# Output of a delta rule: products and sums on VectorE alone, loop written out

## The chip, the cores and the metric

One core of a Trainium2 chip runs the whole program. The metric is the device time of one execution in microseconds (us). An engine is named as in the profile: PE is TensorE, DVE is VectorE, ACT is ScalarE, POOL is GpSimd, SP is the queue that starts DMAs.

## What is computed

The program is a chain of four layers, each a mixer and a feed-forward part, over 4096 tokens of 128 channels. The change touches the last mixer only, a delta rule with 16 heads of 64 channels over a sequence of 4 steps (S = 4, indices t and r below) for each of 1024 positions (8 tiles j of 128 partitions). Cut to what matters, the reference does

```
def step(W, inp):
    q_t, k_t, v_t, b_t = inp
    v_old = jnp.einsum('bhd,bhdv->bhv', k_t, W)
    new_v = b_t * (v_t - v_old)
    W = W + jnp.einsum('bhd,bhv->bhdv', k_t, new_v)
    out_t = jnp.einsum('bhd,bhdv->bhv', q_t, W)
    return (W, out_t)
_, outs = lax.scan(step, W0, (qs, ks, vs, bs))
out = SCALE * out / (denominator + EPS)
attn_out = jnp.einsum('sbi,oi->sbo', layer_out, W_o)
x = h + attn_out
```

Since the recurrence has only four steps, the kernel doesn't keep W. It first computes coefficients alpha[t, r] for each token and head from dot products of queries and keys, and then the output of step t as the sum over r <= t of alpha[t, r] times the value v[r]. The last part, values, weighted sums, projection by W_o and the addition to h, is the stage called "out".

## The kernel before: the stage "out"

The work is 8 turns j (JT = 8), one for each tile of 128 partitions, and in each turn 4 units t (S = 4). Sizes: a value tile v[r] is 128 x 1024 fp32 (16 heads x 64).

- Values: TensorE multiplies XT by wv, two matmuls of 512 columns for each r (line 2155), into the PSUM tiles pv; ScalarE copies each into v (line 2186).
- Sums: for unit t, VectorE multiplies v[0] by alpha[t, 0] into acc (line 2223). GpSimd multiplies v[r] by alpha[t, r] for r = 1 to t into the two-deep tile tmp (line 2142), and VectorE adds each product to acc (line 2231). Each of these covers 128 x 1024 elements. In a turn there are 4 first products, 6 products on GpSimd and 6 additions.
- Turn: TensorE transposes acc in 8 pieces into pt (line 2160), ScalarE copies them to lT (line 2194), two copies of 512 columns.
- Projection: TensorE multiplies lT by woT in 8 accumulating matmuls into po (line 2172), and VectorE adds po to its rows of XN, which hold h (line 2213, the helper `finish`).

The loops over j are hardware loops (`Fori`). [...] The helper `pipelined` calls `prepare(j + 1)` ahead of `rest(j)`. Each engine runs its own list in order. In `rest`, TensorE does turn(0), and then for each t turn(t + 1) and the projection of t; all values of the next turn are computed in one block ahead of that. xj for the next turn is copied only when the earlier turn is nearly finished: both the copy and ScalarE's eviction wait with

```
pool.wait_ge(x_done, j * S + (S + 1))
```

while VectorE's additions wait for GpSimd, and GpSimd for a free half of tmp:

```
dve.wait_ge(tmp_ready, j * NPAIR + (k + 1))
pool.wait_ge(ch, j * NPAIR + (k + 1))
```

VectorE does `finish(t - 2)` after the sum of t, and after the last unit of a turn `finish(S - 2)` and `finish(S - 1)`, before it starts the next turn.

Of the kernel before, what the change touches and what calls it, by code (L numbers as in the profile page):

```python
# [15 lines left out]
ALU = mybir.AluOpType  # L16
# [1698 lines left out]
def delta_rule(nc, X, XN, XT, ident, W_qkvb, W_o, ln_g, ln_b):  # L1715
# [30 lines left out]
    with Stage(nc, "delta") as s:  # L1746
# [351 lines left out]
        with Stage(nc, "out") as s1:  # L2098
            v = s1.sb("v", [P, 2, S, NH, D_])
            xj = s1.sb("xj", [P, 2, S, P])  # L2100
            aj = s1.sb("aj", [P, 2, S, S, NH])
            acc = s1.sb("acc", [P, 2, NH, D_])
            tmp = s1.sb("tmp", [P, 2, NH, D_])
# [4 lines left out]
            xj_ready, aj_ready, v_mm, v_ready, tmp_ready, acc_ready, t_mm, lT_ready, out_mm, x_done, ch, chm = (s1.sem(n) for n in (  # L2108
                "xj_ready", "aj_ready", "v_mm", "v_ready", "tmp_ready", "acc_ready", "t_mm", "lT_ready", "out_mm", "x_done", "additions", "firsts"))
            NPAIR = S * (S - 1) // 2  # L2110

            def pipelined(eng, prepare, rest):

                prepare(0, 0)
                with eng.Fori(0, JT // 2 - 1) as j2:
                    for par in range(2):
                        prepare(j2 * 2 + (par + 1), 1 - par)
                        rest(j2 * 2 + par, par)
                prepare(JT - 1, 1)
                rest(JT - 2, 0)  # L2120
                rest(JT - 1, 1)

            with nc.Block() as block:

                @block.gpsimd
                def _(pool):
                    def prepare(j, par):

                        pool.wait_ge(x_done, j * S + (S + 1))
                        nc.gpsimd.tensor_copy(xj[:, par].unsqueeze(2), XTj[:, :, bass.ds(j, 1), :]).then_inc(xj_ready, 1)  # L2130
                        nc.gpsimd.tensor_copy(aj[:, par].rearrange("p t s h -> p (t s) h").unsqueeze(2),
                                              alpha[:].rearrange("p t s j h -> p (t s) j h")[:, :, bass.ds(j, 1), :]).then_inc(aj_ready, 1)

                    def rest(j, par):
                        pool.wait_ge(aj_ready, j + 1)
                        k = 0
                        for t in range(1, S):
                            for r in range(1, t + 1):
                                pool.wait_ge(v_ready, j * 2 * S + (2 * r + 4))

                                pool.wait_ge(ch, j * NPAIR + (k + 1))
                                nc.gpsimd.tensor_tensor(tmp[:, k % 2], v[:, par, r], bcast(aj[:, par, t, r], D_), ALU.mult).then_inc(tmp_ready, 1)
                                k += 1

                    pipelined(pool, prepare, rest)

                @block.tensor
                def _(pe):
                    def prepare(j, par):
                        pe.wait_ge(xj_ready, j + 1)  # L2150
                        for t in range(S):
                            for half in range(2):

                                pe.wait_ge(v_ready, j * 2 * S + (2 * t + half + 1))
                                nc.tensor.matmul(pv[half][:], xj[:, par, t], wv[:, half * GROUP:(half + 1) * GROUP], start=True, stop=True).then_inc(v_mm, 1)

                    def turn(j, t):
                        pe.wait_ge(acc_ready, j * S + (t + 1))
                        for a in range(HD // P):
                            ins = nc.tensor.transpose(pt[t % 2][a // 4][:, (a % 4) * P:(a % 4 + 1) * P],  # L2160
                                                      acc[:, t % 2].rearrange("p h d -> p (h d)")[:, a * P:(a + 1) * P], ident[:])
                        ins.then_inc(t_mm, 1)

                    def rest(j, par):
                        turn(j, 0)
                        for t in range(S):
                            if t + 1 < S:
                                turn(j, t + 1)
                            pe.wait_ge(lT_ready, j * S + (t + 1))
                            pe.wait_ge(x_done, j * S + (t + 2 * S))  # L2170
                            for a in range(HD // P):
                                ins = nc.tensor.matmul(po[t % 2][:, 0:C], lT[:, t % 2, a], woT[:, a], start=(a == 0), stop=(a == HD // P - 1))
                            ins.then_inc(out_mm, 1)

                    pipelined(pe, prepare, rest)

                @block.scalar
                def _(act):
                    act.sem_inc(v_ready, 2)
                    def prepare(j, par):  # L2180

                        act.wait_ge(x_done, j * S + (S + 1))
                        for t in range(S):
                            for half in range(2):
                                act.wait_ge(v_mm, j * 2 * S + (2 * t + half + 1))
                                nc.scalar.activation(v[:, par, t, half * 8:(half + 1) * 8].rearrange("p h d -> p (h d)"), pv[half][:], ACT.Copy).then_inc(v_ready, 1)
# [376 lines left out]
```

## Time and profile before

| what | value |
|---|---|
| median of 3 runs | 4349.28 us (4348.84 to 4349.62) |
| the profiled execution | 4347.39 us |
| its span, first to last instruction | 4345.1 us |
| granted TensorE clock, mean | 0.851 of full speed |
| busy in the span: PE / DVE / ACT / POOL | 3053.7 / 2461.8 / 1169.1 / 912.8 us |
| stretch of the stage "out" in the trace | 3614.2 to 3871.9 us from the span's start |
| busy in that stretch: PE / DVE / ACT / POOL | 169.36 / 146.65 / 72.39 / 134.96 us |

The program runs stage by stage with a barrier of all engines between them, so a stage's length adds straight to the time. The profiled execution lies 2.2 us above its span and 1.9 us below the median. Times in the trace count from the span's start. "Idle before" is time in which the engine stood still ahead of the instructions of a row, and the arrow names what ended it.

### The profile page before, as it was taken

The numbers are of one execution on the slowest core, as the hardware profiler recorded it, in microseconds if no ns is written. First come the engines' busy times: TensorE is split into PE (matmuls) and PEld (weight loads), VectorE is DVE, ScalarE is ACT, GpSimd is POOL, SyncE is SP. The second block draws the span as 40 slices with busy tenths as digits, with TensorE's granted clock in tenths as the row PEclk, the third lists the DMA queues.
The fourth block names the chain that finished last, engine by engine and source line by source line (L and its number), as shares of the span: only waits on it lengthen the run. The fifth ranks groups of instructions, "written<-read, shape, count | busy, mean of one in ns | idle before, by whom it ended". The sixth has DMA issues, their size and how long they took to land. (4 is left out here: it accounts for less than half of the span.)

```text
span 4345.1 us, 37123 instructions
## 1 busy us (share of the span) xinstructions
PE 3053.7 (70%) x10599; PEld 1669.7 (38%) x10607; DVE 2461.8 (57%) x4267; ACT 1169.1 (27%) x1861; POOL 912.8 (21%) x521
## 2 busy tenths in 40 slices
PE   1003499799999749999687767458989975635654
PEld 0002256455555524444344423234444433433221
DVE  6785433422222377777544570257777846666876
ACT  1001233211111113333333103234444422212420
POOL 0000000000000000000132111238989853520000
PEclk7556699899999879999787798769999987876888
DMA  0000000000000146455000201110000000000000
GB/s 24 0 0 0 20 0 0 15 0 0 0 0 0 42 74 143 135 143 136 4 1 0 61 8 50 44 39 0 0 0 1 0 20 0 0 2 0 0 5 19
DMA packets 93888, 107.16 MB, mean 25 GB/s; under 512 B 20555, under 2 KB 54476, under 8 KB 93516
## 3 DMA queue, kind: packets, MB, share of 16 engines
q1 hardware_dynamic: 91724, 101.65, 9.5%
q0 software_dynamic: 2048, 4.20, 0.3%
q8 instruction: 45, 0.74, 0.1%
q14 instruction: 71, 0.58, 0.0%
HBM read 91.78 MB, written 14.02 MB: 24 GB/s over the span
## 5 line engine op out<-in xcount | busy, mean ns | idle before, releaser
L1846 POOL TENSOR_TENSOR dots_pr<-dots_g 128x1536 f32<-128x1536 f32 (+1 forms) x129 | 394.2, 3098 | 122.1 <-DVE dots_g L1951 78.3
L1872 PE MATMUL dots_fold<-dots_pr,all_ident 128*128 128x512 f32 x688 | 325.0, 619 | 2.7 <-ACT dots_pr L1912 2.7
L670 DVE SCALAR_TENSOR_TENSOR attn_sim<-attn_sc,attn_mask 128x512 f32<-128x512 f32 (+3 forms) x256 | 125.9, 492 | 316.9 <-PE attn_sc L600 313.7
L600 PE MATMUL attn_sc<-attn_q,attn_xb 128*128 128x512 f32 (+3 forms) x768 | 295.0, 486 | 0.0
L611 PE MATMUL attn_op<-attn_sim,attn_v 128*128 128x512 f32 (+3 forms) x768 | 295.0, 486 | 0.0
L243 PE MATMUL mix_po<-mix_woT,mix_y 128*128 128x128 f32 x128 | 25.5, 390 | 366.7 <-DVE mix_y L357 366.7
L778 PE MATMUL grp_po<-grp_h,grp_down 128*128 128x512 f32 x512 | 263.2, 596 | 10.2 <-DVE grp_h L888 10.2
L786 PE MATMUL grp_ph<-all_xt,grp_up 128*128 x512 | 261.4, 596 | 1.1 <-ACTq L808 1.1
L1948 DVE TENSOR_TENSOR dots_m<-dots_pu,dots_sg 128x512 f32<-128x512 f32 x256 | 164.7, 686 | 161.3 <-ACT dots_sg L1903 154.5
L816 ACT ACTIVATE grp_r<-grp_ph 128x512 f32<-128x512 f32 x272 | 162.7, 598 | 310.8 <-PE grp_ph L786 298.2
L883 DVE TENSOR_TENSOR grp_t<-grp_r,grp_cb 128x512 f32<-128x512 f32 x256 | 177.2, 692 | 90.5 <-ACT grp_r L816 79.0
L1912 ACT ACTIVATE dots_pr<-dots_pr 128x1536 f32<-128x1536 f32 (+1 forms) x129 | 169.5, 1339 | 158.2 <-POOL dots_pr L1846 158.2
L1859 PE MATMUL dots_pu<-delta_wE,all_xt 128*128 128x264 f32 x512 | 152.2, 429 | 80.6 <-DVE dots_g L1951 79.0
L1846 POOL TENSOR_TENSOR all_xn<-dots_g 128x1536 f32<-128x1536 f32 (+3 forms) x63 | 195.7, 3148 | 18.3 <-PE dots_fold L1872 18.3
L1872 PEld LDWEIGHTS dots_fold<-dots_pr,all_ident 128*128 128x128 f32 x688 | 137.0, 199 | 147.3 <-issue 141.8
L600 PEld LDWEIGHTS attn_sc<-attn_q,attn_xb 128*128 128x128 f32 x768 | 141.0, 190 | 125.7 <-issue 107.1
L888 DVE TENSOR_TENSOR grp_h<-grp_t,grp_r 128x512 f32<-128x512 f32 x256 | 177.0, 692 | 10.2
L611 PEld LDWEIGHTS attn_op<-attn_sim,attn_v 128*128 128x128 f32 x768 | 141.0, 190 | 98.4 <-issue 68.9
L243 PEld LDWEIGHTS mix_po<-mix_woT,mix_y 128*128 128x128 f32 x128 | 24.7, 301 | 370.0 <-issue 370.0
L1859 PEld LDWEIGHTS dots_pu<-delta_wE,all_xt 128*128 128x128 f32 x512 | 102.1, 208 | 164.2 <-DVE dots_g L1951 120.3
L1951 DVE SCALAR_TENSOR_TENSOR dots_g<-dots_m,dots_pu 128x512 f32<-128x512 f32 x256 | 163.4, 680 | 0.0
L1872 PE MATMUL dots_fold<-all_xn,all_ident 128*128 128x512 f32 x336 | 155.9, 608 | 1.2 <-ACT all_xn L1912 1.2
(596 smaller groups left out, 5599.2 us busy)
## 6 DMA issues: line engine op xcount, KB each, us to landing
grp_cb<-grp_combine SPq DMA_DIRECT2D x512, 128.0 KB, 3.2
cap_xs<-cap_zero SPq DMA_DIRECT2D x7, 320.0 KB, 4.3
experts_xe<-cap_xs SPq DMA_DIRECT2D x7, 320.0 KB, 3.3
cap_w<-in_L_ffn_W_dram SPq DMA_DIRECT2D x1, 2048.0 KB
cap_ys<-experts_yo SPq DMA_DIRECT2D x8, 256.0 KB, 2.3
delta_h<-all_xn SPq DMA_DIRECT2D x1, 2048.0 KB
all_xn<-delta_h SPq DMA_DIRECT2D x1, 2048.0 KB, 8.0
out_dram<-all_x SPq DMA_DIRECT2D x1, 2048.0 KB, 8.7
```

What stands on the lines that cost most here:

```text
L600: nc.tensor.matmul(sc[k % SC][:, 0:w], xb[:, m * P:(m + 1) * P], q[:, par, n0:n0 + w], start=True, stop=True).then_inc(s_mm, 1)
L611: ins = nc.tensor.matmul(op[half][:, n0 - half * GROUP:n0 - half * GROUP + w], v[:, par, m], sim[:, par, k, 0:w], start=False, stop=False)
L778: ins = nc.tensor.matmul(po[par][:], w, h[:, (par * NJ + j) % HB], start=(j == 0), stop=(j == NJ - 1))
L786: nc.tensor.matmul(ph[j % 2][:], w, XT[:, bass.ds(g * GROUP, GROUP)], start=True, stop=True).then_inc(up_mm, 1)
L883: tt(t_[:, j % 2], r[:, j % 2], cb[:, j % CB], ALU.mult).then_inc(tch, 1)
L888: tt(h[:, (par * NJ + j) % HB], a[:, j % 2], r[:, j % 2], ALU.mult).then_inc(h_done, 1)
L1846: nc.gpsimd.tensor_tensor(slot[U % SLOTS][:, r0 + i0:r0 + i0 + n], g[:, I % 2, a0:a0 + n, hs], key, ALU.mult).then_inc(pp_ready, 1)
L1859: ins = nc.tensor.matmul(heads(n % 2)[:, q * HQ:(q + 1) * HQ], XTj[:, k // 2, j], wE[:, 1 - k % 2, h0:h0 + HQ], start=True, stop=True)
L1872: ins = nc.tensor.matmul(fold[U % NU][:].rearrange("p (n h f) -> p n h f", h=HQ, f=FW), ident[:], slot[U % SLOTS][:, :, :, f * FW:(f + 1) ...
L1912: nc.scalar.activation(v_, v_, ACT.Relu).then_inc(relu_done, 1)
L1948: tt(m[:, sh], x[..., sh + 1:sh + 1 + D_], sg[:, n % 2], ALU.mult).then_inc(m_ready, 1)
L1951: ins = stt(g[:, I % 2, k, :, sh * D_:(sh + 1) * D_], m[:, sh], 0.0, x[..., 0:D_], ALU.max, ALU.mult)
```

## The change

GpSimd has no work left in the stage: VectorE makes all ten products of a turn from v and alpha directly. For a unit t it first issues the product with v[0] into acc, then all products r = 1 to t into a three-deep tile `part`, and then the additions. The loops over j are written out, so that TensorE reads XT and VectorE reads alpha in place (xj and aj are gone), and every wait compares with a constant. The values of turn j + 1 are no longer a block: two of their matmuls stand behind the transposes of each unit, and the projection of the unit before comes behind those. ScalarE follows the same order. VectorE's `finish(n - 2)` follows each unit n = 4j + t, across the border of turns.

The diff, with the removed loops cut:

```diff
             v = s1.sb("v", [P, 2, S, NH, D_])
-            xj = s1.sb("xj", [P, 2, S, P])
-            aj = s1.sb("aj", [P, 2, S, S, NH])
             acc = s1.sb("acc", [P, 2, NH, D_])
-            tmp = s1.sb("tmp", [P, 2, NH, D_])
+            part = s1.sb("part", [P, S - 1, NH, D_])
...
-                @block.gpsimd
-                def _(pool):
...
-                        nc.gpsimd.tensor_copy(xj[:, par].unsqueeze(2), XTj[:, :, bass.ds(j, 1), :]).then_inc(xj_ready, 1)
...
-                                nc.gpsimd.tensor_tensor(tmp[:, k % 2], v[:, par, r], bcast(aj[:, par, t, r], D_), ALU.mult).then_inc(tmp_ready, 1)
...
                 @block.tensor
                 def _(pe):
+                    def values(j, t):
+                        if j >= JT:
+                            return
+                        for half in range(2):
+                            n = (j * S + t) * 2 + half
+                            if n >= 2:
+                                pe.wait_ge(v_ready, n - 1)
+                            nc.tensor.matmul(pv[half][:], XTj[:, t, j], wv[:, half * GROUP:(half + 1) * GROUP], start=True, stop=True).then_inc(v_mm, 1)
+
+                    def sums(j, t):
+                        n = j * S + t
+                        if n >= 2:
+                            pe.wait_ge(lT_ready, n - 1)
+                        pe.wait_ge(acc_ready, n + 1)
                         for a in range(HD // P):
                             ins = nc.tensor.transpose(pt[t % 2][a // 4][:, (a % 4) * P:(a % 4 + 1) * P],
...
+                    def project(n):
+                        if n < 0:
+                            return
+                        pe.wait_ge(lT_ready, n + 1)
+                        if n >= 2:
+                            pe.wait_ge(x_done, n - 1)
+                        for a in range(HD // P):
+                            ins = nc.tensor.matmul(po[n % 2][:, 0:C], lT[:, n % 2, a], woT[:, a], start=(a == 0), stop=(a == HD // P - 1))
+                        ins.then_inc(out_mm, 1)
+
+                    for t in range(S):
+                        values(0, t)
+                    for j in range(JT):
                         for t in range(S):
...
+                            sums(j, t)
+                            values(j + 1, t)
+                            project(j * S + t - 1)
+                    project(JT * S - 1)
...
                 @block.vector
...
+                    def finish(n):
+                        if n < 0:
+                            return
+                        j, t = divmod(n, S)
+                        dve.wait_ge(out_mm, n + 1)
+                        xt = XN[:, j + t * JT]
+                        tt(xt, po[n % 2][:, 0:C], xt, ALU.add).then_inc(x_done, 1)
+
                     dve.wait_ge(h_in, 16)
...
+                    for j in range(JT):
+                        for t in range(S):
+                            n = j * S + t
+                            dve.wait_ge(v_ready, 2 * (n + 1))
+                            if n >= 2:
+                                dve.wait_ge(t_mm, n - 1)
+                            ins = tt(acc[:, n % 2], v[:, j % 2, 0], bcast(alpha[:, t, 0, j], D_), ALU.mult)
+                            ins.then_inc(acc_first if t else acc_ready, 1)
+                            if n >= 1:
+                                dve.wait_ge(acc_ready, n)
+                            for r in range(1, t + 1):
+                                tt(part[:, r - 1], v[:, j % 2, r], bcast(alpha[:, t, r, j], D_), ALU.mult).then_inc(part_ready, 1)
+                            for r in range(1, t + 1):
+                                k = j * NPART + t * (t - 1) // 2 + r
+                                if r == 1:
+                                    dve.wait_ge(acc_first, j * (S - 1) + t)
                                 else:
...
+                                    dve.wait_ge(added, j * (NPART - S + 1) + (t - 1) * (t - 2) // 2 + r - 1)
+                                dve.wait_ge(part_ready, k)
+                                ins = tt(acc[:, n % 2], acc[:, n % 2], part[:, r - 1], ALU.add)
+                                ins.then_inc(added if r < t else acc_ready, 1)
+                            finish(j * S + t - 2)
+                    finish(JT * S - 2)
+                    finish(JT * S - 1)
```

VectorE's list before, units t = 2 and t = 3 of a turn (out_acc is acc, out_tmp is the product made by GpSimd, all_xn is XN, REGISTER_ALU computes a value to wait for):

```order
L2223 TENSOR_TENSOR out_acc<-out_v,out_aj 128x1024
L2228 REGISTER_ALU
L2230 REGISTER_ALU
L2231 TENSOR_TENSOR out_acc<-out_acc,out_tmp 128x1024
L2234 REGISTER_ALU
L2231 TENSOR_TENSOR out_acc<-out_acc,out_tmp 128x1024
L2234 REGISTER_ALU
L2213 ISA
L2213 TENSOR_TENSOR all_xn<-out_po,all_xn 128x128
```

One product by VectorE stands ahead of the two additions of t = 2, and the finish of an earlier unit behind them.

The same list after the change, from unit t = 3 of one turn to unit t = 1 of the next (out_part is part, delta_alpha is alpha):

```order
L2195 TENSOR_TENSOR out_acc<-out_v,delta_alpha 128x1024
L2200 TENSOR_TENSOR out_part<-out_v,delta_alpha 128x1024 x3
L2208 TENSOR_TENSOR out_acc<-out_acc,out_part 128x1024 x3
L2186 TENSOR_TENSOR all_xn<-out_po,all_xn 128x128
L2195 TENSOR_TENSOR out_acc<-out_v,delta_alpha 128x1024
L2186 TENSOR_TENSOR all_xn<-out_po,all_xn 128x128
L2195 TENSOR_TENSOR out_acc<-out_v,delta_alpha 128x1024
L2200 TENSOR_TENSOR out_part<-out_v,delta_alpha 128x1024
L2208 TENSOR_TENSOR out_acc<-out_acc,out_part 128x1024
L2186 TENSOR_TENSOR all_xn<-out_po,all_xn 128x128
```

Four products stand ahead of three additions, and unit t = 0 is one product between two finishes.

TensorE's list before, in one turn, from the last value matmul:

```order
L2155 MATMUL out_pv<-delta_wv,out_xj 128x512
L2158 ISA
L2160 MATMUL out_pt<-all_ident,out_acc 128x128 x8
L2158 REGISTER_ALU
L2160 MATMUL out_pt<-all_ident,out_acc 128x128 x8
L2170 REGISTER_ALU
L2172 MATMUL out_po<-delta_woT,out_lT 128x128 x8
```

Here no value matmul stands between transposes and projections. After the change each unit repeats three rows:

```order
L2129 MATMUL out_pt<-all_ident,out_acc 128x128 x8
L2121 MATMUL out_pv<-delta_wv,all_xt 128x512 x2
L2140 MATMUL out_po<-delta_woT,out_lT 128x128 x8
L2129 MATMUL out_pt<-all_ident,out_acc 128x128 x8
L2121 MATMUL out_pv<-delta_wv,all_xt 128x512 x2
```

The projection of a unit now stands behind the transposes of the next unit and two value matmuls.

## Rows read from the trace of the kernel before

**Rows 1.** Groups by line, 3614.3 to 3871.9: count | busy us, mean ns | idle.

```profile
L2142 POOL TENSOR_TENSOR out_tmp<-out_v,out_aj 128x1024 f32<-128x1024 f32 x48 | 118.7, 2486 | 60.0 <-DVE out_acc L2231 53.9 <-ACT out_v L2186 6.1
L2231 DVE TENSOR_TENSOR out_acc<-out_acc,out_tmp 128x1024 f32<-128x1024 f32 x48 | 84.8, 1767 | 30.5 <-POOL out_tmp L2142 28.6
L2223 DVE TENSOR_TENSOR out_acc<-out_v,out_aj 128x1024 f32<-128x1024 f32 x32 | 53.1, 1678 | 26.1 <-PE out_pt L2160 17.8 <-ACT out_v L2186 6.6 <-DVE all_xn L2213 1.3
L2213 DVE TENSOR_TENSOR all_xn<-out_po,all_xn 128x128 f32 x32 | 9.3, 292 | 53.0 <-PE out_po L2172 48.6 <-DVE out_acc L2231 4.4
```

**Rows 2.** Waits in the same stretch: us in total, times, longest us.

```profile
PE out_pv L2155 <- POOL out_xj L2130: 64.6, 7, 53.7
DVE all_xn L2213 <- PE out_po L2172: 48.6, 16, 5.1
DVE out_acc L2231 <- POOL out_tmp L2142: 28.6, 15, 2.2
```

**Rows 3.** The tile out_acc: durations of one, min/median/max in ns.

```profile
L2231 DVE TENSOR_TENSOR out_acc<-out_acc,out_tmp x48: 1224/1226/2908, 3625.0 to 3861.4; 128x1024 f32<-128x1024 f32 x48
```

**Rows 4.** Timeline, stage start: start us, us, engine, line, tile [idle <-releaser].

```profile
3615.26 0.61 POOL L2130 COPY out_xj<-all_xt 128x512 f32<-128x512 f32 x1 [76.15 <-DVEq L2203]
3615.93 16.21 PE L2155 MATMUL out_pv<-delta_wv,out_xj 128*128 128x512 f32 x32 [53.67 <-POOL out_xj L2130]
3620.21 1.23 DVE L2223 TENSOR_TENSOR out_acc<-out_v,out_aj 128x1024 f32<-128x1024 f32 x1 [5.98 <-ACT out_v L2186]
```

**Rows 5.** Timeline, one turn j of the loop.

```profile
3717.48 2.77 DVE L2223 TENSOR_TENSOR out_acc<-out_v,out_aj 128x1024 f32<-128x1024 f32 x2
3720.48 0.60 ACT L2186 ACTIVATE out_v<-out_pv 128x512 f32<-128x512 f32 x1 [7.05 <-PE out_pv L2155]
3721.34 0.60 ACT L2186 ACTIVATE out_v<-out_pv 128x512 f32<-128x512 f32 x1 [0.26 <-PE out_pv L2155]
3731.60 1.09 PE L2160 MATMUL out_pt<-all_ident,out_acc 128*128 128x128 f32 x8 [0.61 <-DVEq L2236]
3731.75 0.29 DVE L2213 TENSOR_TENSOR all_xn<-out_po,all_xn 128x128 f32 x1 [0.27 <-DVE out_acc L2231]
3731.96 2.37 DVE L2223 TENSOR_TENSOR out_acc<-out_v,out_aj 128x1024 f32<-128x1024 f32 x1
3732.53 1.95 PE L2172 MATMUL out_po<-delta_woT,out_lT 128*128 128x128 f32 x16
3741.63 1.97 PE L2160 MATMUL out_pt<-all_ident,out_acc 128*128 128x128 f32 x8 [7.15 <-DVEq L2236]
3743.39 4.67 PE L2172 MATMUL out_po<-delta_woT,out_lT 128*128 128x128 f32 x32
3748.21 0.29 DVE L2213 TENSOR_TENSOR all_xn<-out_po,all_xn 128x128 f32 x1 [1.49 <-PE out_po L2172]
3748.93 1.43 DVE L2223 TENSOR_TENSOR out_acc<-out_v,out_aj 128x1024 f32<-128x1024 f32 x1 [0.43 <-DVE all_xn L2213]
```

**Rows 6.** Timeline of VectorE: two or more operations close together.

```profile
3843.15 2.36 DVE L2223 TENSOR_TENSOR out_acc<-out_v,out_aj 128x1024 f32<-128x1024 f32 x2
...
3634.39 2.49 DVE L2231 TENSOR_TENSOR out_acc<-out_acc,out_tmp 128x1024 f32<-128x1024 f32 x2
```

**Rows 7.** Two stretches: busy by engine, then PEclk (the granted clock), DMA share, GB/s.

```profile
3852.80:3855.50 2.70, 2.70 (x24) 2.60 (x24) 2.60 (x3) 1.09 (x2) 2.70 (x2) 1.00 0.00 0
4094.30:4096.80 2.50, 2.50 (x8) 0.30 (x8) 2.50 (x7) 0.50 (x2) 0.00 (x0) 0.50 0.00 0
```

**Rows 8.** Timeline of TensorE after shorter idles.

```profile
3852.72 1.09 PE L2160 MATMUL out_pt<-all_ident,out_acc 128*128 128x128 f32 x8 [2.85 <-DVEq L2236]
...
4094.24 2.11 PE L2351 MATMUL sink_cp<-sink_ahead,sink_pick 128*8 128x512 bf16 x5 [4.06 <-DVE sink_ahead L2412]
```

**Rows 9.** Timeline, end of the stage.

```profile
3861.40 1.23 DVE L2231 TENSOR_TENSOR out_acc<-out_acc,out_tmp 128x1024 f32<-128x1024 f32 x1 [1.86 <-POOL out_tmp L2142]
3870.17 0.29 DVE L2213 TENSOR_TENSOR all_xn<-out_po,all_xn 128x128 f32 x1 [1.59 <-PE out_po L2172]
```

More of the change, by code:

```diff
@@ L2107, in delta_rule @@
             po = [s1.ps(f"po{k}") for k in range(2)]
[L2108 to L2121, printed above, removed]
@@ L2123, in delta_rule @@
[L2123 to L2145 removed]
+            v_mm, v_ready, acc_first, part_ready, added, acc_ready, t_mm, lT_ready, out_mm, x_done = (s1.sem(n) for n in (
+                "v_mm", "v_ready", "acc_first", "part_ready", "added", "acc_ready", "t_mm", "lT_ready", "out_mm", "x_done"))
@@ L2147, in _ @@
+            NPART = S * (S - 1) // 2
+            with nc.Block() as block:
                 @block.tensor
                 def _(pe):
[L2149 to L2155, printed above, removed]
@@ L2162, in turn @@
                         ins.then_inc(t_mm, 1)
-                    def rest(j, par):
-                        turn(j, 0)
-                        for t in range(S):
[L2167 to L2173, printed above, removed]
@@ L2188, in rest, with take @@
-                    def rest(j, par):
-                        for t in range(S):
-                            act.wait_ge(t_mm, j * S + (t + 1))
-                            act.wait_ge(x_done, j * S + (t + 2 * S))
+                    def take(j, t):
+                        if j >= JT:
+                            return
+                        for half in range(2):
+                            act.wait_ge(v_mm, (j * S + t) * 2 + half + 1)
+                            if j >= 2:
+                                act.wait_ge(acc_ready, S * (j - 1))
+                            nc.scalar.activation(v[:, j % 2, t, half * 8:(half + 1) * 8].rearrange("p h d -> p (h d)"), pv[half][:], ACT.Copy).then_inc(v_ready, 1)
@@ L2193, in rest @@
+                    for t in range(S):
+                        take(0, t)
+                    for j in range(JT):
+                        for t in range(S):
+                            n = j * S + t
+                            act.wait_ge(t_mm, n + 1)
+                            if n >= 2:
+                                act.wait_ge(out_mm, n - 1)
                             for half in range(2):
@@ L2195, in rest @@
                             ins.then_inc(lT_ready, 1)
-                    pipelined(act, prepare, rest)
+                            take(j + 1, t)
                 @block.vector
```

52 lines of the change are left out of this document (7 added, 45 removed).

## The prediction, written before the changed kernel ran

> **What bounds the kernel now.** The stages run one after another behind barriers, so I look only at the stage "out". First the groups of instructions by line in its stretch [rows 1]: VectorE is busy for 84.8 + 53.1 + 9.3 = 147.2 us and stands idle for 30.5 + 26.1 + 53.0 = 109.6 us, together 256.8 us. No engine is full; GpSimd has 118.7 us of products and waits for VectorE between them. Second the waits [rows 2]: VectorE waits 48.6 us for projections and 28.6 us for GpSimd's products, and TensorE waits for the copy xj, but the 53.7 us in that row lie ahead of the stage. Third the durations of the tile acc [rows 3]: one addition takes 1224 ns at best and mostly 1226 ns, yet their mean is 1767 ns [rows 1] and the longest is 2908 ns. The long ones lie beside products of GpSimd. So both engines work on the same tiles in turns, and each addition costs more than the work in it. A turn j lasts 3748.93 - 3717.48 = 31.5 us [rows 5].
>
> **What goes.** GpSimd's 48 products (118.7 us busy) and 16 copies, with VectorE's 28.6 us of waits for them, and the stretching of VectorE's operations: (1767 - 1226) ns x 48 = 26.0 us and, with the same 1226 ns for the first products, (1678 - 1226) ns x 32 = 14.5 us. The copy xj also goes from the start: it began at 3615.26 and the first value matmul at 3615.93 [rows 4], so VectorE's first operation moves from 3620.21 to 3619.5.
>
> **What comes.** 48 products on VectorE. The trace has no product by VectorE of r > 0, but the first product has the same operands, shape and type, and costs 1.23 us undisturbed [rows 4]. Consecutive operations overlap at their ends. Two that don't depend on each other took 2.36 us together [rows 6], so the second began 2.36 - 1.23 = 1.13 us after the first. Two dependent additions took 2.49 us [rows 6], a step of 1.26 us. A finish takes 0.29 us and the next operation starts 0.21 us after it (3731.75 to 3731.96) [rows 5]. Now the turn on VectorE: 16 large operations, of which 4 must wait for the one just ahead (the addition of t = 1, the second of t = 2, the second and third of t = 3), since the products stand first. That is 12 x 1.13 + 4 x 1.26 + 4 x 0.21 = 19.4 us.
>
> **TensorE's side of a turn.** The work stays the same, only its order changes. Eight transposes occupy 0.93 us (3731.60 to 3732.53), a projection takes 1.95 us, of which the last 0.16 us overlap with what follows, so 1.79 us, and one value matmul 0.86 us (ScalarE's evictions at 3720.48 and 3721.34) [rows 5]. A unit is 0.93 + 1.72 + 1.79 = 4.44 us, a turn 17.8 us, under VectorE's 19.4. But the new order makes VectorE wait in two places. Let A be the end of the last addition of t = 3. A hand-over between engines takes about 0.15 us (3743.39 + 4.67 = 3748.06 to 3748.21) [rows 5].
> - Unit t = 0 of the next turn: VectorE's finish(t = 1) and one product end their slots at A - 0.10 + 0.21 + 1.13 = A + 1.24. Then it wants the projection of t = 2, which stands behind the transposes of t = 3 and two value matmuls: A + 0.15 + 0.93 + 1.72 + 1.95 + 0.15 = A + 4.90. It waits 3.7 us, and all of unit t = 1 is queued behind that wait.
> - Unit t = 1: VectorE reaches its finish(t = 3) at 4.90 + 0.21 + 1.13 + 1.26 + 1.13 = A + 8.63. TensorE was free at A + 4.59 and needs 0.93 + 1.72 + 1.95 + 0.15 more: A + 9.34. It waits 0.7 us.
> - Units t = 2 and 3 last 5.8 and 8.4 us, longer than TensorE's 4.44, and don't wait.
>
> A turn is then 19.4 + 3.7 + 0.7 = 23.8 us at TensorE's full clock. ScalarE's four copies of a unit (0.60 us each [rows 5]) lie beside all this, and so do its waits. The registers and branches of the loops cost nothing that I count: the steps above are measured with them in between.
>
> **TensorE's clock.** During t = 3 TensorE has 4.44 us of work in VectorE's 8.38 us, so it idles for 3.9 us in each turn. Before, after an idle of 7.15 us the eight transposes took 1.97 us instead of 1.09 [rows 5]: the lower of the two levels, 1.2 GHz. After 2.85 us they took 1.09 us at a granted clock of 1.00; after 4.06 us the granted clock was 0.50 [rows 7, 8]. 3.9 us is nearest to the last, so I expect it to be low in most turns, though not in all. What then lies on the path to the first wait is 0.93 + 1.72 = 2.65 us of transposes and values that last twice as long. Bounds for a turn: 0, and 4.44 us if the projection is slow too. I take 2.65 us in two turns of three, over 7 turns: 12.4 us.
> The Trainium skill ("TensorE: Matmul & The Clock Gate", on HAM oscillation in real kernels) warns that short bursts of matmuls between waits let the clock fall again in every tile, which speaks against spreading the values out. By that rule all seven turns are slow; it would add 6 us to the sum, and the trace agrees as far as the 4.06 us row goes.
>
> **The sum,** for the profiled execution (4347.39 us). VectorE starts at 3619.5. The first turn has two finishes fewer, and about 1.1 us of waits for values and transposes: 19.4 - 0.4 + 1.1 = 20.1. Six turns of 23.8: 142.8. The last turn has no values of a next one behind its transposes, so no second wait: 23.1. After A the end is what it was, two projections at a low clock: (3870.17 + 0.29) - (3861.40 + 1.23) = 7.8 [rows 9]. Together 3813.3, with the clock 3825.7. The stage ended at 3870.46, so 44.8 us go: 4302.6 us. The median shown is 1.9 us above the profiled execution, so I predict 4304 us for the median. Nothing in earlier or later stages is touched.
>
> **Rivals.**
> - *The clock holds.* If 3.9 us of idle isn't enough, the 12.4 us and about 2.6 us of the tail go too: 4304 - 15 = 4289. For it: the 2.85 us row. Against it: the 4.06 us row. If instead all of a unit is slow in all seven turns, it is 4.44 x 7 = 31.1 instead of 12.4 us: 4323.
> - *Products first gain nothing.* If each operation waited until the one before had finished, all 12 independent steps would cost 1.26 instead of 1.13 us: 8 x 12 x 0.13 = 12.5 us, 4316. Against it: the pair of 2.36 us, though it is one of few undisturbed ones. The Trainium skill states this as its rule ("VectorE: DVE Perf Modes", section "The DRAIN you can't avoid": the pipe empties before the next operation starts, with or without a semaphore); this trace doesn't agree, since 2.36 us is less than 2 x 1.23.
> - *The work only moves.* VectorE's other waits, 109.6 - 30.5 = 79.1 us, could all stay, because the projections come later than now: 128 x 1.23 + 9.3 + 79.1 = 245.8 instead of 256.8 us, 11 us less, 4338. For it: 48.6 us of waits for projections, the largest wait, and in the new order each projection stands behind the next unit's sum. Against it: the waits before came mostly from the two finishes at the end of each turn, which drained the pipeline, and from the block of values.
> - *TensorE becomes the bound, and it is slower than before.* The values, so far a dense block, are cut into pairs with idle between them. Should the clock stay at its low level throughout, a unit costs 8.9 us on TensorE, a turn 35.5 us instead of 31.5, and the stage 8 x 35.5 plus the tail 7.8 = 292 against 255 us from 3615.2: 37 us slower, 4386. It decides at about 17.8 / 31.5 = 0.56 of full clock. For it: 7.15 us of idle brought the low level. Against it: it came back inside the next 4.67 us row (32 matmuls of which the second 16 were at full speed), and all but one idle are now shorter.
>
> **Chances.** Forecast (some turns slow) 0.60; the clock holds 0.18; no gain from products first 0.13; the work only moves 0.06; TensorE bound 0.03. A difference within 0.2% of 4349 us, 8.7 us, is what a measurement of this kernel can't tell from no change. "The work only moves" gives 11 us, and I put half of it inside that bound. Faster 0.60 + 0.18 + 0.13 + 0.03 = 0.94, same 0.03, slower 0.03. The range goes from the case in which the clock holds, with 3 us for the small waits, to the one in which every unit after an idle is slow: 4286 to 4324. It leaves out the last two rivals and the ends of the first three.
>
> **What would show it.** GpSimd has no rows in the stage. All large operations of VectorE take about 1.23 us, products in groups a step of 1.13 apart. The longest waits of VectorE are seven or more of 3.7 us, or 6 to 8 where the clock is low, at the finish that follows the lone product of t = 0; those at t = 1 are under 1 us; waits for value tiles occur in the first turn only. TensorE's transposes of t = 3 take 1.97 us in most turns. A turn lasts 24 to 27 us and the stage about 210. The prediction is wrong if VectorE's operations are longer than 1.3 us, if waits appear at every unit, or if TensorE has hardly any idle.

## The result and the profile after

| | before | changed |
|---|---|---|
| median, runs on one chip | 4349.06 us (4347.44 to 4349.62, 4 runs) | 4302.27 us (4298.68 to 4303.53, 4 runs) |
| ratio to before, 95% interval | | 0.9894 [0.9882, 0.9906] |
| the profiled execution / its span | 4347.39 / 4345.1 us | 4303.53 / 4301.8 us |
| mean granted TensorE clock | 0.851 | 0.853 |

The change is 46.8 us faster, where 45 us were forecast (4304 us; the time lies inside the range of 4286 to 4324). The chips differ (the kernel before took 4324.8 us on one of them), so every experiment below is compared by its ratio to the kernel before on its own chip; the changed kernel measured a second time that way gave 0.9899 [0.9884, 0.9914]. These intervals reach 4 to 7 us to each side, so smaller differences between two experiments are read from the length of the stage in the traces, given in a table behind experiment 9.

The groups by line of the changed kernel, in the stretch of the stage (count | busy us, mean ns | idle before, and what ended it):

```profile
L2208 DVE TENSOR_TENSOR out_acc<-out_acc,out_part 128x1024 f32<-128x1024 f32 x48 | 58.7, 1223 | 2.0 <-DVE out_part L2200 0.5
L2200 DVE TENSOR_TENSOR out_part<-out_v,delta_alpha 128x1024 f32<-128x1024 f32 x48 | 56.5, 1218 | 0.0
L2195 DVE TENSOR_TENSOR out_acc<-out_v,delta_alpha 128x1024 f32<-128x1024 f32 x32 | 38.9, 1217 | 6.4 <-ACT out_v L2161 5.9 <-PE out_pt L2129 0.2 <-issue 0.2
L2186 DVE TENSOR_TENSOR all_xn<-out_po,all_xn 128x128 f32<-128x128 f32 x32 | 9.2, 288 | 46.7 <-PE out_po L2140 46.4
```

Against [rows 1]: GpSimd's row is gone. VectorE has 48 operations more, but its three large groups are now 58.7 + 56.5 + 38.9 = 154.1 us where two groups took 137.9. An addition takes 1223 ns instead of 1767, a first product 1217 instead of 1678. VectorE's idle time, 109.6 us before, is 55.1.

The chain of waits (who waited for whom: us in total, times, longest us):

```profile
DVE all_xn L2186 <- PE out_po L2140: 46.4, 13, 6.0
...
DVE out_acc L2195 <- ACT out_v L2161: 5.9, 2, 5.4
```

Against [rows 2], the 28.6 us for GpSimd's products are gone and the 48.6 us for projections are almost all still there: 46.4. They only fall elsewhere. One turn and its neighbours on VectorE (start us, us, instruction, [idle before <-releaser]):

```profile
3620.28 1.23 DVE L2195 TENSOR_TENSOR out_acc<-out_v,delta_alpha 128x1024 f32<-128x1024 f32 x1 [5.44 <-ACT out_v L2161]
...
3657.17 1.22 DVE L2195 TENSOR_TENSOR out_acc<-out_v,delta_alpha 128x1024 f32<-128x1024 f32 x1
3658.30 3.49 DVE L2200 TENSOR_TENSOR out_part<-out_v,delta_alpha 128x1024 f32<-128x1024 f32 x3
3661.71 3.74 DVE L2208 TENSOR_TENSOR out_acc<-out_acc,out_part 128x1024 f32<-128x1024 f32 x3
3665.36 0.28 DVE L2186 TENSOR_TENSOR all_xn<-out_po,all_xn 128x128 f32<-128x128 f32 x1
3665.56 1.22 DVE L2195 TENSOR_TENSOR out_acc<-out_v,delta_alpha 128x1024 f32<-128x1024 f32 x1
3672.79 0.29 DVE L2186 TENSOR_TENSOR all_xn<-out_po,all_xn 128x128 f32<-128x128 f32 x1 [6.02 <-PE out_po L2140]
...
3677.10 0.29 DVE L2186 TENSOR_TENSOR all_xn<-out_po,all_xn 128x128 f32<-128x128 f32 x1 [0.42 <-PE out_po L2140]
...
3826.03 0.29 DVE L2186 TENSOR_TENSOR all_xn<-out_po,all_xn 128x128 f32<-128x128 f32 x1 [1.71 <-PE out_po L2140]
```

The lone product of t = 0 starts at 3665.56, and then VectorE stands still for 6.02 us, until the projection of t = 2 is there. At t = 1 it waits 0.42 us (so in four of seven turns, in the others not at all), at t = 2 and 3 it doesn't wait. There are seven of the long waits: 4.86, 6.02, 4.90, 6.04, 4.91, 6.04 and 4.91 us, 37.7 us together. TensorE at the same place:

```profile
3657.20 1.06 PE L2129 MATMUL out_pt<-all_ident,out_acc 128*128 128x128 f32 x8 [1.67 <-DVE out_acc L2208]
...
3665.59 1.94 PE L2129 MATMUL out_pt<-all_ident,out_acc 128*128 128x128 f32 x8 [3.83 <-DVE out_acc L2208]
3667.32 3.58 PE L2121 MATMUL out_pv<-delta_wv,all_xt 128*128 128x512 f32 x4
3670.74 1.95 PE L2140 MATMUL out_po<-delta_woT,out_lT 128*128 128x128 f32 x16
```

Two stretches of it, in t = 3 of this turn and in t = 2 of the next (busy us of PE, weight loads, DVE, ACT and POOL, then the granted clock, DMA share, GB/s):

```profile
3665.60:3670.00 4.40, 4.40 (x12) 2.85 (x13) 1.18 (x2) 1.68 (x3) 0.00 (x0) 0.50 0.00 0
3684.00:3690.00 6.00, 3.90 (x24) 2.75 (x22) 5.97 (x6) 2.17 (x4) 0.00 (x0) 1.00 0.00 0
```

After an idle of 3.83 us the eight transposes take 1.94 us instead of 1.06 and the four records of the two value matmuls 3.58 instead of 1.88; the granted clock is 0.50 there and 1.00 in t = 2. All seven turns show transposes of 1.94 us. The values alternate between 3.6 us (slow to their end) and 2.4 to 2.5 us (slow in part), which makes waits of 6.0 and 4.9 us.

### The profile page after: what moved, and what is told of

Its sections match the earlier page's. It is cut to its first block and busy times, and to the rows that moved or that the text cites. A ratio compares the mean times of both kernels' runs of the same rounds, so it can differ in the third digit from the quotient of the medians.

```text
span 4301.8 us, 36726 instructions
## 1 busy us (share of the span) xinstructions
PE 3047.9 (71%) x10599; PEld 1668.8 (39%) x10607; DVE 2472.3 (57%) x4315; ACT 1166.3 (27%) x1861; POOL 778.0 (18%) x457
## 5 line engine op out<-in xcount | busy, mean ns | idle before, releaser
L1948 DVE TENSOR_TENSOR dots_m<-dots_pu,dots_sg 128x512 f32<-128x512 f32 x256 | 164.7, 685 | 161.3 <-ACT dots_sg L1903 154.1
L888 DVE TENSOR_TENSOR grp_h<-grp_t,grp_r 128x512 f32<-128x512 f32 x256 | 177.1, 692 | 10.2
```

The source lines that it names most:

```text
L888: tt(h[:, (par * NJ + j) % HB], a[:, j % 2], r[:, j % 2], ALU.mult).then_inc(h_done, 1)
L1948: tt(m[:, sh], x[..., sh + 1:sh + 1 + D_], sg[:, n % 2], ALU.mult).then_inc(m_ready, 1)
```

## The experiments

**1. Products first, undone.** Each product stands right before its own addition:

```diff
                             for r in range(1, t + 1):
                                 tt(part[:, r - 1], v[:, j % 2, r], bcast(alpha[:, t, r, j], D_), ALU.mult).then_inc(part_ready, 1)
-                            for r in range(1, t + 1):
                                 k = j * NPART + t * (t - 1) // 2 + r
```

> The changed kernel (4302 us), but VectorE makes each product right before its own addition, so that all 6 additions of a turn wait for the operation just ahead of them instead of 4. Theory (steps of 1.13 us where operations don't depend on each other, 1.26 us where they do): 2 x 0.13 us more in a turn, 2 us in all, 4304 us. Rival (the products standing first are a main part of the gain, or the pipe drains at every dependence for longer): 1 us or more for each of the 48 additions, 4312 us or more. Rival (the drain comes always, products first buys nothing): 4302 us, and all steps equal.

Measured: 4296.37 us, ratio 0.9887 [0.9870, 0.9903], against 0.9894 for the change. The time excludes the second expectation (4312 us or more), but with these intervals it can't tell the other two apart. The steps in the trace fit neither of them. The steps of VectorE (its timeline, unit t = 2 of one turn):

```profile
3649.77 1.21 DVE L2195 TENSOR_TENSOR out_acc<-out_v,delta_alpha 128x1024 f32<-128x1024 f32 x1
3650.90 1.22 DVE L2200 TENSOR_TENSOR out_part<-out_v,delta_alpha 128x1024 f32<-128x1024 f32 x1
3652.22 1.23 DVE L2207 TENSOR_TENSOR out_acc<-out_acc,out_part 128x1024 f32<-128x1024 f32 x1
3653.36 1.22 DVE L2200 TENSOR_TENSOR out_part<-out_v,delta_alpha 128x1024 f32<-128x1024 f32 x1
3654.69 1.22 DVE L2207 TENSOR_TENSOR out_acc<-out_acc,out_part 128x1024 f32<-128x1024 f32 x1
```

An addition starts 1.32 us after the product it needs (3650.90 to 3652.22), a product 1.14 us after an unrelated addition (3652.22 to 3653.36). So a dependence costs 0.19 us between product and addition, more than the 0.13 us that I had from two additions, and a turn of VectorE's own work grows by 0.59 us: this part had the right sign and less than half the size. That is 4.7 us in eight turns, yet the stage in the trace is 4.1 us shorter than in the changed kernel (201.95 against 206.04 us). That comes from the waits: those for projections fell from 46.4 to 37.2 us.

```profile
3671.76 0.29 DVE L2186 TENSOR_TENSOR all_xn<-out_po,all_xn 128x128 f32<-128x128 f32 x1 [5.79 <-PE out_po L2140]
...
3695.96 0.29 DVE L2186 TENSOR_TENSOR all_xn<-out_po,all_xn 128x128 f32<-128x128 f32 x1 [3.49 <-PE out_po L2140]
...
3770.28 0.29 DVE L2186 TENSOR_TENSOR all_xn<-out_po,all_xn 128x128 f32<-128x128 f32 x1 [5.18 <-PE out_po L2140]
```

Of the seven long waits of the stage four are 3.49 us, near what the steps give at full clock (3.66), and three are 4.99 to 5.79. Ahead of each of the four short ones TensorE was slow one unit earlier, at t = 2: three times its transposes there took 1.43 to 1.94 us instead of 1.06, once the values behind them 3.50 instead of 1.88.

**2. The products to VectorE, everything else as before.** Loops, copies and the order of TensorE and ScalarE stay:

```diff
-            tmp = s1.sb("tmp", [P, 2, NH, D_])
+            tmp = s1.sb("tmp", [P, S - 1, NH, D_])
...
+                                for r in range(1, t + 1):
+                                    tt(tmp[:, r - 1], v[:, par, r], bcast(aj[:, par, t, r], D_), ALU.mult).then_inc(tmp_ready, 1)
```

> The kernel before (4349 us) with its loops, copies and order on TensorE and ScalarE, and only the products moved from GpSimd to VectorE, products first. Theory A (the order of TensorE is at least half of it: the block of 8 value matmuls lets VectorE's unit t = 2 start only 10.2 us after a turn begins, and the last two finishes drain the turn for 7.4 us): 10.2 + 0.2 + 5.8 + 0.3 + 8.4 + 7.4 = 32.3 us a turn against 31.5, so 4349 to 4356 us, no gain at all. Theory B (the gain is GpSimd's waits and the stretched operations, 69 us, less the added products): 4305 to 4315 us.

Measured: 4346.90 us, ratio 1.0001 [0.9991, 1.0011]. Theory A. VectorE's operations are fast, and the time is what it was:

```profile
3721.39 2.77 DVE L2215 TENSOR_TENSOR out_acc<-out_v,out_aj 128x1024 f32<-128x1024 f32 x2
3724.08 1.41 DVE L2221 TENSOR_TENSOR out_tmp<-out_v,out_aj 128x1024 f32<-128x1024 f32 x1
...
3731.56 1.23 DVE L2215 TENSOR_TENSOR out_acc<-out_v,out_aj 128x1024 f32<-128x1024 f32 x1 [4.80 <-PE out_pt L2152]
...
3751.87 0.29 DVE L2205 TENSOR_TENSOR all_xn<-out_po,all_xn 128x128 f32 x1 [5.09 <-PE out_po L2164]
3753.94 0.29 DVE L2205 TENSOR_TENSOR all_xn<-out_po,all_xn 128x128 f32 x1 [1.78 <-PE out_po L2164]
3754.66 2.76 DVE L2215 TENSOR_TENSOR out_acc<-out_v,out_aj 128x1024 f32<-128x1024 f32 x2 [0.43 <-DVE all_xn L2205]
```

This turn takes 3754.66 - 3721.39 = 33.3 us, the longest but for the first; the six between the first and the last take 30.3 to 33.3 us, 31.5 on average, as before the change and 0.8 us less than worked out. After t = 1 VectorE waits for the transposes, which stand behind eight value matmuls; unit t = 2 begins 10.2 us into this turn, as worked out, and 8.8 us into every second one. At its end the two finishes wait 5.09 and 1.78 us.

**3. The new order, with GpSimd's products.**

```diff
+                @block.gpsimd
+                def _(pool):
...
+                                nc.gpsimd.tensor_tensor(part[:, k % 2], v[:, j % 2, r], bcast(alpha[:, t, r, j], D_), ALU.mult).then_inc(part_ready, 1)
```

> The changed kernel (4302 us) with its written-out loops and order, but GpSimd makes the products r > 0 into a two-deep tile, as before. Theory A (order is the larger part; GpSimd and VectorE block each other, 6 x 1.9 + 10 x 1.22 = 23.6 us a turn plus some of the wait for the projection): a turn of 25 to 28 us, 4300 to 4325 us, VectorE's operations again up to 2.9 us long. Theory B (GpSimd's part is the whole gain): about 4345 us.

Measured: 4317.69 us, ratio 0.9932 [0.9915, 0.9948]. Theory A again: the time lies in its 4300 to 4325 us. The groups by line:

```profile
L2122 POOL TENSOR_TENSOR out_part<-out_v,delta_alpha 128x1024 f32<-128x1024 f32 x48 | 124.3, 2601 | 168.8 <-DVE out_acc L2219 86.3 <-ACT out_v L2174 82.5
L2219 DVE TENSOR_TENSOR out_acc<-out_acc,out_part 128x1024 f32<-128x1024 f32 x48 | 86.9, 1810 | 19.4 <-POOL out_part L2122 16.8
```

The additions take 1810 ns, as before the change (1767), and GpSimd's products 2601 ns. Still 30 us of the 46 are there. With experiment 2 this makes a square, on one scale (4348 us for before): order alone -30 us, VectorE alone 0 us, both -46 us. "Order" stands here for all that came with it: TensorE's and ScalarE's lists, VectorE's finish across the border of turns, the written-out loops, and the end of GpSimd's copies xj and aj (the turn's slices of XT and alpha). No run takes these apart. The move off GpSimd is worth nothing while the old order sets the turn, and 16 us once it doesn't.

**4. GpSimd beside, for nobody.** The changed kernel with 48 products of the same shape on tiles of GpSimd's own; it shares only alpha with VectorE, and both only read it:

```diff
+                                pool.wait_ge(gp, max(k - 1, 1))
+                                nc.gpsimd.tensor_tensor(idle[:, 1 + k % 2], idle[:, 0], bcast(alpha[:, t, r, j], D_), ALU.mult).then_inc(gp, 1)
```

> The changed kernel (4302 us) plus 48 products on GpSimd of the same shape as before, on tiles of its own; nobody reads them and nobody but GpSimd waits for them. Theory (both engines block each other at the same tiles' memory, whatever data they work on): VectorE's 128 x 1024 operations are stretched again, mean 1.6 us or more instead of 1.22, and the time rises by 40 to 90 us, to 4340 to 4390 us. Rival (the long operations before came from waiting for each other's data): VectorE's operations stay at 1.22 us, 4302 us.

Measured: 4379.15 us, ratio 1.0074 [1.0057, 1.0091], 77 us more than the change. The groups by line:

```profile
L2223 DVE TENSOR_TENSOR out_acc<-out_acc,out_part 128x1024 f32<-128x1024 f32 x48 | 97.6, 2033 | 2.0 <-DVE out_part L2215 0.5
L2215 DVE TENSOR_TENSOR out_part<-out_v,delta_alpha 128x1024 f32<-128x1024 f32 x48 | 97.4, 2067 | 0.0
L2210 DVE TENSOR_TENSOR out_acc<-out_v,delta_alpha 128x1024 f32<-128x1024 f32 x32 | 38.8, 1214 | 6.7 <-ACT out_v L2176 6.5 <-issue 0.2
```

Nobody waits for GpSimd here, and VectorE's additions and products take 2033 and 2067 ns. The first products, which GpSimd waits for before it starts, stay at 1214. VectorE loses 97.6 + 97.4 - 58.7 - 56.5 = 79.8 us to 48 operations, 1.66 us for each. GpSimd's 48 products take 2812 to 2881 ns here; in the kernel before the shortest took 1896 ns, the mean 2486 [rows 1] (durations of one, min/median/max in ns):

```profile
L2142 POOL TENSOR_TENSOR out_tmp<-out_v,out_aj x48: 1896/2874/2942, 3622.1 to 3858.4; 128x1024 f32<-128x1024 f32 x48
```

The timeline of this run shows how they meet:

```profile
3657.75 1.22 DVE L2215 TENSOR_TENSOR out_part<-out_v,delta_alpha 128x1024 f32<-128x1024 f32 x1
3657.91 2.82 POOL L2123 TENSOR_TENSOR out_idle<-out_idle,delta_alpha 128x1024 f32<-128x1024 f32 x1 [12.27 <-DVE out_acc L2210]
3659.07 2.74 DVE L2223 TENSOR_TENSOR out_acc<-out_acc,out_part 128x1024 f32<-128x1024 f32 x1
```

VectorE's product began first and keeps its 1.22 us. GpSimd's ends at 3660.73, 1.76 us after the end of that one, and VectorE's addition, begun in between, ends 1.08 us after GpSimd's. Each of the two looks as if it did its own work only once the other was through. So the long operations before need no wait for data to explain them: while one engine works on SBUF tiles this way, the other stands inside its own instruction. The Trainium skill has it so ("SBUF — State Buffer", section "SBUF: two separate sides": the port pair that both share is locked by one of them for a whole instruction, and the loser blocks fully); the trace agrees, with 1.66 us lost to one GpSimd product and the three rows above.

**5. TensorE kept busy.** Eight matmuls that nobody reads, in the idle of t = 3:

```diff
                             project(j * S + t - 1)
+                            if t == 2:
+                                for a in range(8):
+                                    nc.tensor.matmul(pt[1][0][:, 0:P], woT[:, a % (HD // P)], ident[:], start=True, stop=True)
```

> The changed kernel (4302 us) plus 8 extra matmuls of 128 columns on TensorE behind the projection in unit t = 2 of each turn, 1.8 us of work into a PSUM tile that nobody reads; they cut its idle ahead of the transposes of t = 3 from 3.9 to about 2.1 us. Theory (the low clock after that idle is the 12 us by which the seven waits at t = 0 exceed 3.66 us each): transposes of t = 3 take 1.06 us instead of 1.94, those waits 3.5 us instead of 4.9 to 6.0, time 4288 to 4292 us. Rival (these waits come from the queue order alone): 4302 us, waits unchanged.

Measured: ratio 0.9865 [0.9849, 0.9882], on a chip where before takes 4324.77 and this kernel 4265.37 us. Against 0.9894 that is 12.6 us at 4349 us, or 4290 us, inside the 4288 to 4292 expected: more work, less time. The two intervals touch, but the stage in the trace says the same: 193.4 us instead of 206.0. VectorE's waits for projections (its timeline, three of the seven turns):

```profile
3620.48 0.29 DVE L2189 TENSOR_TENSOR all_xn<-out_po,all_xn 128x128 f32<-128x128 f32 x1 [3.49 <-PE out_po L2140]
...
3669.38 0.29 DVE L2189 TENSOR_TENSOR all_xn<-out_po,all_xn 128x128 f32<-128x128 f32 x1 [5.16 <-PE out_po L2140]
...
3763.82 0.29 DVE L2189 TENSOR_TENSOR all_xn<-out_po,all_xn 128x128 f32<-128x128 f32 x1 [3.49 <-PE out_po L2140]
```

Six of seven are 3.49 us, and the one of 5.16 is the turn whose transposes of t = 3 still took 1.94 us. In two other turns the low level moved to the transposes of t = 2 (1.79 and 1.51 us), where VectorE doesn't wait for it. The total of all waits for projections is 33.7 us instead of 46.4, and the difference, 12.7 us, is the measured one: 11.6 us at t = 0 and 1.1 us behind the last unit.

**6. The projection ahead of the values.** The two calls in TensorE's loop change places:

```diff
                             sums(j, t)
-                            values(j + 1, t)
                             project(j * S + t - 1)
+                            values(j + 1, t)
```

> The changed kernel (4302 us) with the projection of the unit before issued ahead of the two value matmuls instead of behind them. By my steps the projection of t = 2 ends at A + 0.15 + 1.8 + 2.7 + 0.15 with the low clock, the wait at t = 0 falls from 5.4 to 3.6 to 4.0 us, and the wait at t = 1 rises to about 1 us: 7 to 10 us less, 4292 to 4295 us. Rival (only the clock matters, whatever stands there is stretched by the same 1.9 us and the values must be done anyway): 4300 us or more. Rival (the whole time of the values goes): 17 us less, 4285 us.

Measured: ratio 0.9858 [0.9841, 0.9874], 4260.90 against 4324.77 us: 15.7 us under the change at 4349 us. I expected 7 to 10, so this is a miss. The long waits are 3.1 to 3.4 us in five of the seven turns, and in those TensorE's transposes of t = 3 took 1.06 to 1.75 us instead of 1.94. In one turn they took 1.94, and the wait is 4.21 us; in one, the whole unit ran at a granted clock of 1.00, and the wait is 1.77 us:

```profile
3753.30 1.06 PE L2129 MATMUL out_pt<-all_ident,out_acc 128*128 128x128 f32 x8 [3.82 <-DVE out_acc L2208]
3754.20 1.95 PE L2140 MATMUL out_po<-delta_woT,out_lT 128*128 128x128 f32 x16
...
3756.26 0.29 DVE L2186 TENSOR_TENSOR all_xn<-out_po,all_xn 128x128 f32<-128x128 f32 x1 [1.77 <-PE out_po L2140]
```

So two things changed at once, the order and where the low clock falls. These waits allow an estimate of the shares. At full clock the wait is 1.77 us here and 3.49 us in experiment 5, 1.72 us less, which is the time of the two value matmuls. In seven turns that is 12.0 us of the 15.3 us by which the long waits fell (37.7 to 22.4 us); the other 3.3 us are the clock. With the 1.1 us by which the waits at t = 1 grew, the order alone comes to 10.9 us, near the upper end of what was expected.

**7. Finish three units behind.** po gets four PSUM tiles and pt two instead of four:

```diff
-                        if n >= 2:
-                            pe.wait_ge(x_done, n - 1)
+                        if n >= 4:
+                            pe.wait_ge(x_done, n - 3)
...
-                            finish(j * S + t - 2)
+                            finish(j * S + t - 3)
```

> The changed kernel (4302 us) with VectorE's finish three units behind instead of two; po has four PSUM tiles, pt half as many. Theory (the waits for projections, 46.4 us in the changed kernel, are the order of VectorE's list and not missing speed of TensorE): the wait moves to unit t = 1 and is about 2.3 us a turn with the low clock, 24 us less, 4278 us. Rival (TensorE bounds the turn): the wait moves elsewhere in full, 4295 us or more.

Measured: 4244.34 us, ratio 0.9814 [0.9798, 0.9830]; a second time, on the chip of the second run of the change, 4269.75 us and 0.9822 [0.9808, 0.9835], 33 us under that run (4302.98 us). That is beyond the 24 us expected. One turn on VectorE:

```profile
3641.37 1.23 DVE L2195 TENSOR_TENSOR out_acc<-out_v,delta_alpha 128x1024 f32<-128x1024 f32 x1 [0.36 <-PE out_pt L2129]
...
3644.78 2.48 DVE L2208 TENSOR_TENSOR out_acc<-out_acc,out_part 128x1024 f32<-128x1024 f32 x2
...
3648.51 3.49 DVE L2200 TENSOR_TENSOR out_part<-out_v,delta_alpha 128x1024 f32<-128x1024 f32 x3
3651.92 3.74 DVE L2208 TENSOR_TENSOR out_acc<-out_acc,out_part 128x1024 f32<-128x1024 f32 x3
...
3661.35 1.23 DVE L2195 TENSOR_TENSOR out_acc<-out_v,delta_alpha 128x1024 f32<-128x1024 f32 x1 [0.36 <-PE out_pt L2129]
```

From 3641.37 to 3661.35 it is 19.98 us, of which 19.4 are the work that I had counted and 0.36 a wait for the transposes of the unit two before, whose tile acc it needs. The waits for projections are 7.9 us in the whole stage, 6.8 of them behind the last unit. I had expected 2.3 us of wait at t = 1 in every turn from a low clock. In the six turns between the first and the last TensorE's longest idle is now 2.28 us, and the transposes behind it took 1.06 us in four of them and 1.94 in two.

**8. Both.**

> Finish three units behind and projection ahead of the values, together. Theory: no wait of VectorE is left in the middle of a turn, a turn is its 19.6 us of work, 38 to 42 us less than the changed kernel: 4260 to 4265 us. Rival (TensorE's 17.8 us at full clock are stretched by the low one beyond 19.6 us and it becomes the bound): waits spread over all units, 4275 us or more.

Measured: 4242.80 us, ratio 0.9815 [0.9798, 0.9831], 34 us under the change and the same as experiment 7, where 38 to 42 us were expected. With hardly a wait for projections left, the place of the projection is off the path. The earlier projection gains nothing, and the values behind it delay the next transposes, on which VectorE waits up to 1.26 us (7.2 us in all, 5.9 in experiment 7).

**9. Alternating again, where VectorE bounds the turn,** beside second runs of the change and of experiment 7.

> The changed kernel as it is, on the same chip as the next two, as their reference: 0.989 of the time of the kernel before.

> The kernel with finish three units behind, and in it each product right before its own addition. In the changed kernel this order made the stage 4 us shorter although VectorE's own steps grew by 0.59 us a turn. Theory (the order of products costs 0.59 us a turn wherever VectorE bounds it; the gain in the changed kernel was a low clock of TensorE that fell on other matmuls): now that VectorE waits for nothing, 8 x 0.59 = 4.7 us slower than the kernel with finish three units behind. Rival (alternating is better in itself, because a product and an addition suit each other): as fast or faster.

> The kernel with finish three units behind, once more, on the same chip as the changed kernel and the one that alternates: 34 us (0.8%) faster than the changed kernel, 4 to 5 us faster than the one that alternates.

Measured on one chip: the change 4302.98 us (0.9899), finish later 4269.75 us (4264.17 to 4272.03, 5 runs), the same with alternating products 4276.51 us (4272.46 to 4276.9, 5 runs), 0.9834 [0.9821, 0.9847]. The two ranges lie 0.4 us apart, though the intervals of the ratios overlap: alternating costs 6.8 us by the medians. The traces show where it goes. An undisturbed turn takes 20.56 us instead of 19.97, the 0.59 us of the steps, 4.7 us in all. The profiled executions lie further apart than the medians, 9.9 us in the stage, and VectorE's waits for projections and transposes, 16.2 us instead of 11.3, make up the rest: the low clock touched four of the six inner turns instead of one. So products first is better by itself, and experiment 1 was fast because of where the low clock fell.

The length of the stage in the profiled executions, from VectorE's first 128 x 1024 operation to the end of its last finish:

| kernel | us |
|---|---|
| before / products on VectorE, old order (2) | 250.3 / 252.7 |
| changed, two runs | 206.0 / 206.4 |
| alternating (1) / GpSimd's products, new order (3) | 202.0 / 220.4 |
| GpSimd beside (4) | 283.8 |
| TensorE kept busy (5) / projection first (6) | 193.4 / 191.2 |
| finish later (7), two runs / both (8) | 172.4, 169.5 / 172.8 |
| finish later, alternating (9) | 179.3 |

## Why the prediction was right

**The time** came out at 4302.3 us for 4304 forecast. The profiled execution, for which the sum was made, took 4303.53 us for 4302.6. By the steps:

| step | predicted | in the profile |
|---|---|---|
| an undisturbed product or addition | 1.23 us | 1.22 |
| step, independent / dependent | 1.13 / 1.26 us | 1.13 / 1.26 between additions, 1.32 from product to addition |
| VectorE's first operation, from the end of the stage before | 0.7 us earlier | 5.98 us became 5.44 |
| wait at t = 0, full clock | 3.66 us | 3.49 (experiment 5) |
| wait at t = 1 | 0.71 us in each of six turns | 0.42 in four, none in the others |
| a turn, full clock | 23.8 us | 23.6 (experiment 5) |
| low clock, all turns | 12.4 us | 37.7 - 7 x 3.49 = 13.3 us |
| tail after the last addition | 7.8 us | (3826.03 + 0.29) - 3818.5 = 7.8 |
| the stage from VectorE's first operation | 3825.7 - 3619.5 = 206.2 us | 3826.32 - 3620.28 = 206.0 |

Three of these deserve a remark. The clock term has the right size with the wrong make-up: I had two turns of three at 2.65 us, and it was seven of seven at 1.4 to 2.5 us, because the clock rose again before or just after the values were done. That the two errors cancel is luck; all seven at 2.65 us would have given 4310 us. The transposes' idle of 3.8 us was indeed nearer to the 4.06 us row than to the 2.85 us one [rows 8]. And the profiled execution gained 43.9 us and not 44.8, mostly since the stages ahead of this one ended 0.6 us later in it.

**The rivals.** The clock didn't hold by itself. Its price was given as 15 us with the tail; experiment 5 gets 12.6 us back with one turn of seven still slow, whose wait is 1.7 us longer than the others. VectorE doesn't let an independent operation wait for the end of the one before: steps of 1.13 us at durations of 1.22 us stand in all turns. The Trainium skill ("VectorE: DVE Perf Modes", section "The DRAIN you can't avoid"), from which the prediction took the contrary rule, itself says that an operation which isn't held back starts earlier, and the trace agrees with that, by 0.09 us. That the work only moves is refuted for the whole, but half of it is true in a way I had not seen: 46.4 of 48.6 us of waits for projections stayed, and what went was GpSimd's part and VectorE's wait for the transposes behind the block of values (17.8 us in [rows 1], now 0.2). TensorE didn't become the bound: it has 17.8 us of work at full clock in a turn that lasts 25.6 us on average.

**What the prediction didn't say:** it listed the removed work under GpSimd (118.7 us busy, 28.6 us of waits, 40.5 us of stretching), which reads as if these paid for the gain. Experiment 2 removes these, all but GpSimd's 16 copies, and gains nothing. The forecast was right because the new turn was worked out from its own order, and not as the old time less what goes.

**Open:** the shares in experiment 6 are an estimate that rests on one turn at full clock. And I didn't try the change without written-out loops, so how much of the 30 us of "order" belongs to them, or to the copies xj and aj, isn't shown. Of the loops' registers and branches only this much is seen: VectorE's steps are the same 1.13 us inside the loops of experiment 2. Nor was it tried whether the old loops could do without xj: elsewhere in this kernel TensorE reads its second operand at a register's index (`XT[:, bass.ds(b * SEQ + half * GROUP, GROUP)]`, line 236), while in this stage XT is the first.

## What to carry to other kernels

Before an operation is moved off a shared or slow engine, draw the turn with each engine's list in order: if a wait behind another engine's queue sets the turn, the move can be worth nothing until that queue is reordered, and the two together can be worth more than their sum (here 46 us against 0 + 30). Spread dense blocks of matmuls over the units they feed, and take results late enough that the wait for them falls behind other work; the latter alone gave 33 us here. Short idles of TensorE have a price of their own, which a change elsewhere can shift by some microseconds in either direction, so differences of 5 us between orders need the trace before they are believed.

## What the runs showed of the hardware that I had not expected

An addition that needs the product just ahead starts 1.32 us after it, where one that needs the addition just ahead starts 1.26 us after that, and an independent one 1.13 us. A product of GpSimd on tiles of its own takes 1.66 us from VectorE. And 1.8 us of matmuls for nobody, in each of eight turns, made the kernel 12.6 us faster: the transposes of t = 3 then ran at TensorE's high clock in six of seven turns.

The length of an idle alone doesn't tell whether the low level comes. In the changed kernel it was there at the end of each of the seven idles of 3.8 to 4.1 us. In experiment 6 it came later after such an idle in several turns, and in one, after 3.82 us, not at all. After 2.87 us the transposes were slow in two of six turns of experiment 9, after 2.28 us in two of six of experiment 7. In experiment 1 it came at 2.16 us of idle in some turns, at the transposes of t = 2 instead of t = 3, where VectorE had work enough to hide it:

```profile
3706.77 1.73 PE L2129 MATMUL out_pt<-all_ident,out_acc 128*128 128x128 f32 x8 [2.16 <-DVE out_acc L2207]
...
3730.98 1.94 PE L2129 MATMUL out_pt<-all_ident,out_acc 128*128 128x128 f32 x8 [2.16 <-DVE out_acc L2207]
```
